# Attention in a gated block: stacks of keys and queries copied inside SBUF instead of through memory

## The reference

```
q = _split_heads(x @ qw + qb)
k = _split_heads(ctx @ kw + kb)
v = _split_heads(ctx @ vw + vb)
scores = jnp.einsum('bqhd,bkhd->bhqk', q, k) / np.sqrt(D // H)
scores = scores + mask
probs = jax.nn.softmax(scores, axis=-1)
out = jnp.einsum('bhqk,bkhd->bqhd', probs, v)
```

## Time and profile before

| | |
|---|---|
| median of three runs | 2051.25 us (2050.09 to 2052.86) |
| time of the profiled execution | 2046.32 us |
| its span | 2044.6 us |
| attention stage | about 60 to 1090 us of the span |
| stores of parts | 64 of 512 KB, median 3.3 us from issue to landing |
| loads of kst and of qst | 192 each of 128 KB, median 4.8 and 5.9 us |

### The profile page before, as it was taken

One profiled execution on the slowest core, in us unless ns is written; L12 is line 12 of the kernel. 1 busy time (PEld: TensorE's weight loads), 2 busy tenths in 40 slices (PEclk: granted clock), 3 DMA queues, 4 the chain that ended last, 5 costly groups with the idle time before them and its releaser, 6 DMA issues. The chain is left out here.

```text
span 2044.6 us, 36356 instructions
## 1 busy us (share of the span) xinstructions
PE 1812.3 (89%) x12326; PEld 1336.8 (65%) x12326; DVE 1461.2 (71%) x2914; ACT 1222.3 (60%) x2305; POOL 1172.0 (57%) x989
## 2 busy tenths in 40 slices
PE   0799799999999999998994999960999999999996
PEld 0455355554555555554542888850999999999996
DVE  5378688888888888786881588882777676676772
ACT  0166576666767667665673554530777777777773
POOL 6533464445646445543335546661687787877875
PEclk8599899999999999998997999975999999999998
DMA  2664455655556656446412222124667667676662
GB/s 90 115 132 97 96 106 110 131 117 115 110 110 110 131 115 120 97 88 118 95 33 75 57 83 92 70 84 142 225 210 235 216 213 221 213 230 220 210 225 39
DMA packets 117005, 270.61 MB, mean 132 GB/s; under 512 B 15802, under 2 KB 49722, under 8 KB 116436
## 3 DMA queue, kind: packets, MB, share of 16 engines
q1 hardware_dynamic: 102516, 249.57, 45.9%
q0 software_dynamic: 14304, 18.72, 4.6%
HBM read 196.50 MB, written 71.73 MB: 131 GB/s over the span
## 5 line engine op out<-in xcount | busy, mean ns | idle before, releaser
L703 DVE TENSOR_REDUCE nraw<-ps 128x1 f32<-128x512 f32 x1024 | 649.4, 684 | 201.7 <-PE ps L850 199.5
L618 ACT ACTIVATE spare<-ps 128x512 f32<-128x512 f32 x1024 | 571.4, 600 | 325.0 <-PE ps L860 320.5
L1748 POOL TENSOR_TENSOR u_lo<-u_f,u_hi 128x256 fp32r<-128x256 f32 x273 | 377.7, 1398 | 145.2 <-ACT u_hi L1782 145.2
L1854 PE MATMUL ps_e<-x_hi,we_hi 128*128 128x256 f32 x1092 | 313.0, 287 | 4.9 <-DVE we_lo L1668 4.9
L1854 PE MATMUL ps_e<-x_lo,we_hi 128*128 128x256 f32 x1092 | 305.9, 280 | 0.0
L1854 PE MATMUL ps_e<-x_hi,we_lo 128*128 128x256 f32 x1092 | 305.9, 280 | 0.0
L850 PE MATMUL ps<-kst,qst 50*128 50x512 f32 x1024 | 273.9, 446 | 36.1 <-DVE nraw L703 32.5
L860 PEld LDWEIGHTS ps<-qst,kst 52*128 52x128 f32 x1024 | 102.5, 186 | 282.7 <-ACT spare L618 189.1
L872 PE MATMUL ps<-spare,vaug 128*32 128x512 f32 x2048 | 279.4, 618 | 0.0
L860 PE MATMUL ps<-qst,kst 52*128 52x512 f32 x1024 | 270.6, 505 | 3.5 <-ACT spare L618 3.2
L1708 DVE TENSOR_TENSOR u_f<-ps_e,silu 128x256 f32<-128x256 f32 x273 | 115.1, 422 | 182.0 <-ACT silu L1813 180.8
(11 more groups left out here) (224 smaller groups left out, 3716.8 us busy)
## 6 DMA issues: line engine op xcount, KB each, us to landing
we_raw<-in_experts_w SPq DMA_DIRECT2D x117, 896.0 KB, 4.9
parts_kept<-parts SPq DMA_DIRECT2D x64, 512.0 KB, 3.3
kst<-parts_kept SPq DMA_DIRECT2D x192, 128.0 KB, 4.8
qst<-parts_kept SPq DMA_DIRECT2D x192, 128.0 KB, 5.9
x_raw<-xs SPq DMA_DIRECT2D x39, 259.0 KB, 2.8
x<-sum_tok SPq DMA_DIRECT2D x16, 512.0 KB, 2.6
x_tok<-x SPq DMA_DIRECT2D x16, 512.0 KB, 3.7
x_tok<-in_x SPq DMA_DIRECT2D x8, 512.0 KB, 4.5
```

Source lines behind the costliest of these rows:

```text
L618: act.activation(probs[:, e % 8], ps[:, score_bank(e, par)], ACT.Exp, scale=SCALE).then_inc(exp_made, 1)
L703: dve.tensor_reduce(nraw[:, g % 2, qt, half, i:i + 1], ps[:, max_bank(m, par)], AX.X, ALU.max, negate=True).then_inc(max_made, 1)
L1748: pool.tensor_tensor(u_lo[:, it], u_f[:, q % UPS], u_hi[:, it].bitcast(F32), ALU.subtract).then_inc(ulo_made, 1)
L1854: ins = pe.matmul(ps[:, q % UPS, c * GR:(c + 1) * GR], left, right, start=m == 0, stop=m == len(terms) - 1)
```

## The change

The store to memory and the semaphores for it go, and with them the 2 MB scratch tensor. A stack is filled from the tile `parts` directly: for each of the three slots, four pairs and two halves of the block one transfer of 16 partitions by 512 (32 KB), 24 for each of the four half stacks of a period, each from 16 partitions of parts to 16 partitions of the stack. GpSimd's next split into parts now waits until the stack has landed; before, it waited until the store had.

```diff
+STACK_DMAS = 16 * 24
...
-            def keep_parts(u, kq, mt):
+            def load_stack(u, par, kq, mt):
                 sp.wait_ge(qk_lo_made, u * 4 + 2 * mt + kq + 1)
-                if positive(u):
-                    sp.wait_ge((k_in, q_in)[kq], 96 * 2 * u)
-                sp.dma_start(scratch["parts"][kq, mt].rearrange("h p n -> p h n"),
-                             parts[:, kq].bitcast(F32)).then_inc((k_out, q_out)[kq], 16)
-
-            def load_stack(u, par, kq, mt):
-                sp.wait_ge((k_out, q_out)[kq], 16 * (2 * u + mt + 1))
                 if positive(2 * u + mt):
-                    sp.wait_ge((k_in, q_in)[kq], 96 * (2 * u + mt))
+                    sp.wait_ge((k_in, q_in)[kq], STACK_DMAS * (2 * u + mt))
                 for slot, part in enumerate(STACKED[kq]):
-                    src = scratch["parts"][kq, mt, part].rearrange("(a h d) n -> h d a n", a=4, h=2)
-                    for half in range(2):
-                        row = BLOCK * half + DH * slot
-                        sp.dma_start(
-                            (kst, qst)[kq][row:row + DH, par, 4 * mt:4 * mt + 4, :].bitcast(F32),
-                            src[half]).then_inc((k_in, q_in)[kq], 16)
+                    for a in range(4):
+                        for half in range(2):
+                            row = BLOCK * half + DH * slot
+                            head = DH * (2 * a + half)
+                            sp.dma_start((kst, qst)[kq][row:row + DH, par, 4 * mt + a, :].bitcast(F32),
+                                         parts[head:head + DH, kq, part, :].bitcast(F32)) \
+                                .then_inc((k_in, q_in)[kq], 16)
...
                 elif kind in ("k", "q"):
                     what = "kq".index(kind)
                     if positive(2 * u + n):
-                        pool.wait_ge((k_out, q_out)[what], 16 * (2 * u + n))
+                        pool.wait_ge((k_in, q_in)[what], STACK_DMAS * (2 * u + n))
...
                 if m % 32 == 0:
-                    pe.wait_ge(k_in, 96 * (2 * u + m // 32 + 1))
-                    pe.wait_ge(q_in, 96 * (2 * u + m // 32 + 1))
+                    pe.wait_ge(k_in, STACK_DMAS * (2 * u + m // 32 + 1))
+                    pe.wait_ge(q_in, STACK_DMAS * (2 * u + m // 32 + 1))
```

More of the change, by code:

```diff
@@ L259, in attention_phase @@
         sem(n) for n in ("tb_mm", "tb_up", "c_hi_made", "c_lo_made"))
-    k_out, q_out, k_in, q_in = (sem(n) for n in ("k_out", "q_out", "k_in", "q_in"))
+    k_in, q_in = (sem(n) for n in ("k_in", "q_in"))
     v_mm, v_made = sem("v_mm"), sem("v_made")
@@ L399, in start @@
                     for kq in range(2):
-                        keep_parts(0, kq, mt)
-                    for kq in range(2):
                         load_stack(0, 0, kq, mt)
@@ L417, in period @@
                     load_mask(u + 1, 1 - par, *after)
-                    keep_parts(u + 1, 0, 0)
-                    keep_parts(u + 1, 1, 0)
                     load_stack(u + 1, 1 - par, 0, 0)
@@ L425, in period @@
                 if after:
-                    keep_parts(u + 1, 0, 1)
                     load_stack(u + 1, 1 - par, 0, 1)
@@ L430, in period @@
                 if after:
-                    keep_parts(u + 1, 1, 1)
                     load_stack(u + 1, 1 - par, 1, 1)
@@ L1909, in build @@
         x1 = nc.dram_tensor("x1", [B, P, QT, D], F32).ap()
-        parts = nc.dram_tensor("parts_kept", [2, KD, 2, P, S], F32).ap()
         maxima = nc.dram_tensor("maxima", [2, P, QT * 32], F32).ap()
         masks = nc.dram_tensor("masks", [2, B + 1, S], F32).ap()
-        scratch = {"x1": x1, "x2": x2, "xs": xs, "out": out, "parts": parts,
+        scratch = {"x1": x1, "x2": x2, "xs": xs, "out": out,
                    "masks": masks, "maxima": maxima}
```

## The result

The changed kernel takes 2370.3 us (median of 4, 2369.7 to 2371.4) against 2051.6 us for the kernel before: ratio 1.1555, 95% interval 1.1535 to 1.1575. The prediction, 2114 us with a range to 2155, had the direction and a fifth of the size: 63 us of 319.

What follows compares the result with a forecast made beforehand. TensorE, busy 89%, was taken as the bound, with late stacks on SyncE's queue as the cost. Normal periods 21.8, start 8.4, x reloads 18.1, hiccups 5 and clock 10 sum to 63.3 us: 2114 us, range 2049 to 2155.

Steps and rivals of the forecast that it cites:

- What bounds the kernel, and what the change can bring: Whole kernel: TensorE, busy 89% of the span, bounds it; stacks are off the path, so removing their memory way gains nothing.
- I take 0.47, the value of the rows that share the 16 partitions: SyncE's queue: each direct copy issues 0.47 us after the last, bounded by 0.29 and 0.48; 11.3 us a stack.
- the start: Before the first score: serial key and query copies, then late first maxima, make the first score 8.4 us later.
- the two periods with x: Second and last-but-two periods: SyncE reaches the store of x 9.2 and 8.9 us later, all on the path; 18.1 us.
- The schedule: Normal period on SyncE: queries land at 24.2 us against slot 15's need of 22.6; mostly 1.9 us lost, sum 21.8 us.
- The term for long issues: Attention stage, SyncE: some eleven hiccups with more issues, half of them without slack, 0.9 us each; 5 us.
- The clock: TensorE after new waits of 1.6 us or more: five dips to half clock taken, 10 us, ends 0 and 28.
- GpSimd's new wait at no cost: GpSimd's split waiting for landed stacks: met for the second keys; for second queries nothing, at most 1 us.
- Hidden: Rival on SyncE's queue: small copies issue every 0.37 us or less, so issues hide; 2050 us, chance 0.13.
- faster: Rival: issue pitch near 0.29 us, start gains 3.5 us, a third of VectorE waits goes; 2037 to 2047, chance 0.05.
- Mild: Rival: pitch 0.42 to 0.44 us or other engines run ahead; mainly start and x periods remain; 2058 to 2080, chance 0.14.
- Copies inside SBUF are slow: Rival in the DMA engines: a transfer takes 0.6 us of all engines, periods grow some 12 us; 2230 us, chance 0.08.

Runs made afterwards that it cites:

- twelve copies: Changed kernel copying only two of four head pairs per stack from the third period on, earlier stacks through memory, output not the reference's: 2052.2 us, ratio 1.0005 against before.
- The trains: Kernel before with trains of 12 transfers added at its end, kernel time not compared; for 16 partitions by 2 KB, 0.64 us an issue inside SBUF, 0.47 from memory.
- The run with eighteen copies: Changed kernel copying only three of four head pairs per stack from the third period on, earlier stacks through memory, output not the reference's: 2132.8 us, ratio 1.039 against before.
- k1 alone: Kernel before with only the second half of the keys copied directly inside SBUF, the other stacks through memory: 2055.8 us, ratio 1.0020.

## Why the prediction was wrong

**What bounds the kernel, and what the change can bring: right.** Nothing waited for the stacks before but TensorE once, 3.6 us at the start; the way through memory was hidden and its removal brought nothing (twelve copies: 1.0005).

**"I take 0.47, the value of the rows that share the 16 partitions": the step that failed.** It measured 0.63. The term was bounded by rows that all have one end in memory, and the upper bound, 0.48, was the largest of those rows, as though the one thing that no row showed, both ends in SBUF, could only make it cheaper. The trains put a number on it: 0.47 from memory, 0.64 from SBUF, all else equal. With 0.63 in the prediction's own sum its terms become 24 us for the start (measured 25.0), 19.5 for the first period (20.3), 49 for the two periods with x (54.6), and 202 for the other twelve (228.9). Together 294 us; with 15 for clock and hiccups that is 2355 on the profiled execution's own scale, where the changed kernel's took 2370.9. So the price explains 246 of the 261 us by which the sum of 63.3 fell short of the spans' 324.6.

**The schedule: right in its places, short in size.** The waits came where they were put: slot 15, the two reloads of x, the start. The run with eighteen copies shows the rest of the error without the price: 82 us against 29 to 54. Trains with a long issue in them (up to 12.7 us instead of 11.3) and the clock are what its trace shows; how much each takes was not separated. The term for long issues was too small: eleven were taken, 0.9 us each, and the changed kernel has 35 issues of stacks and maxima of more than 1 us in the stage, some 27 us over the median in all, where the kernel before had seven.

**The clock: undersized.** Five dips of 2 us were taken. With eighteen copies eleven of fourteen waits in slot 15 were followed by 3 to 10 us at half clock; in the changed kernel all fifteen (9.5 to 11.9 us long) were, for 3.5 to 12.8 us behind their end. From the first exponential of the first period to that of the last the mean granted clock is 0.83 (128 to 1370 us), before 0.97 (103 to 1041 us). TensorE's busy time grew by 77.9 us over the whole span for the same matmuls; some of it lies in stretches where TensorE would have waited anyway.

**GpSimd's new wait at no cost: right for the queries**, by their second tile, within 7 us. It was forecast to be met at once and was in fact long (187.8 us in all), behind stacks that landed late. For the keys (126.0 us) it wasn't tested alone; with k1 alone, and with twelve copies a stack, it cost nothing.

**The rivals.** *Hidden* (0.37 us or less) and *faster* fall. *Mild* falls. *Copies inside SBUF are slow* came nearest in time (2230) with a wrong mechanism: it wanted the DMA engines full, and they are 0.22 busy. The change can be too dear by its issues and not by its data, and no rival had an issue that costs more than any row.

**The issue beside the transfer.** The Trainium skill, "DMA: Bandwidth & Descriptors", section "Issuing engines are not separate DMA queues", calls the issue usually small beside the transfer; here 0.63 us of SyncE stand beside 32 KB that keep the engines busy a fifth of that time, so the trace disagrees for small transfers. The 512 cycles per copy in the table of the same page of the Trainium skill, by the prediction's estimate 0.43 us, fit loads and stores of 16 partitions (0.42 us) but neither two partitions (0.25) nor two ends of one kind (0.59).

## What to carry to other kernels

Splitting one large transfer into many small ones moves the cost from the DMA engines to the queue that issues them: multiply the issues by the pitch of a train with the same two kinds of ends, place the sum against the next need on that queue, and measure the pitch first if no row has those ends. A transfer that is hidden pays nothing back when it gets shorter, and its replacement need only be late by a few microseconds in each period to cost the wait and the slower clock behind it. When a price has no row of its own, an end taken from the largest row of another kind is no upper bound.

## What the runs showed of the hardware

- In a train of its kind an issue from SyncE comes 0.62 to 0.68 us after the one before when both ends are in SBUF (1 to 16 partitions of 2 KB, and 16 of 256 B) or both in memory (16 rows of 2 KB); with one end of each kind 0.29 (2 partitions), 0.34 (8), 0.45 to 0.47 (16). ScalarE's one train, 16 partitions inside SBUF, was like SyncE's (0.64).
- When the two kinds alternate, neither keeps its time: 0.55 to 0.57 us behind a copy inside SBUF, 0.62 or 0.63 behind a load.
- With the DMA engines full (0.99 to 1.05) some issues hold SyncE longer: 1.24 us for copies of 128 KB inside SBUF, 0.64 for stores of 256 KB; twelve loads of 128 KB from memory stayed at 0.42.
- An issue from GpSimd costs 0.49 us for 16 partitions from SBUF and 0.48 from memory: for copies inside SBUF it is cheaper than SyncE's.
- Copies of 128 KB between two sets of 16 partitions go at 1.29 us each once the engines are full, 102 GB/s; loads of that shape go at 114 GB/s.
